# A graph-network kernel: three units of a weight combination are moved, one stage's tile order is changed, and the first loads are dealt out anew

## The reference, cut to what matters

```python
h = relu(layernorm(x)); x = x + gnn0(h, edges)          # attention, o, ff1, ff2
h = relu(layernorm(x)); x = x + gnn1(h, edges)          # lin, 2 x (sum neighbours, c1, c2)
h = relu(layernorm(x)); x = x + leaky(norm_adj @ (h @ W) + b)          # GCN
h = relu(layernorm(x)); x = x + rgcn(relu(rgcn(h)))     # relational, two layers
# in rgcn: w = einsum('rb,bio->rio', att, basis)        # 30 bases of 512x512 -> 2 weights, per layer
#          msgs_r = sigmoid(x_j @ gate_r) * x_j @ w[r];  out = segment_sum(...) + x @ root + bias
```

## Time and profile before

| | |
|---|---|
| median of 3 runs | 458.7 us (457.14 to 459.46) |
| the profiled execution | 456.62 us, its span from first to last instruction 454.8 us |
| busy in the span | PE 438.6 us, DVE 346.3, ACT 243.7, POOL 42.9 |
| granted TensorE clock, mean | 1.000 |

### The profile page before, as it was taken

How to read it: one execution, slowest core, us unless ns; L and a number is a source line. 1 busy time by engine, 2 the same in 40 slices (tenths; PEclk the granted TensorE clock), 3 DMA queues, 4 the chain that set the end, 5 groups by cost and what they waited for, 6 DMA issues and landing times.

```text
span 454.8 us, 6200 instructions
## 1 busy us (share of the span) xinstructions
PE 438.6 (96%) x2226; PEld 274.3 (60%) x2226; DVE 346.3 (76%) x736; ACT 243.7 (54%) x428; POOL 42.9 (9%) x59
## 2 busy tenths in 40 slices
PE   8999999899997899999999999999998999999997
PEld 3334554443432346768776866677465788888885
DVE  5999996899999968688779657675759695866212
ACT  5999994676897617543345436544534623511210
POOL 3240000024223011000010000010000000000000
PEclk9999999999999999999999999999999999999999
DMA  7997347426699859978099766777973550000002
GB/s 254 415 398 176 110 174 308 179 93 219 235 380 353 295 206 332 409 272 345 11 372 404 295 246 251 275 252 267 375 199 115 225 186 1 1 0 2 0 3 92
DMA packets 18090, 99.22 MB, mean 218 GB/s; under 512 B 2959, under 2 KB 3599, under 8 KB 7567
## 3 DMA queue, kind: packets, MB, share of 16 engines
q1 hardware_dynamic: 13191, 72.72, 43.4%
q0 software_dynamic: 4000, 25.18, 15.1%
q10 hardware_dynamic: 864, 0.86, 0.6%
HBM read 93.50 MB, written 5.25 MB: 217 GB/s over the span
## 4 chain that ended last, share of the span: by engine, by line
PE 70%; DVE 12%; DMA 8%; issue 8%; ACT 1%; POOL 0%; DVEq 0%; POOLq 0%
PE bank L1371 15%; PE sbank L1703 10%; PE bank L1716 6%; PE sbank L1357 6%; PE sbank L1427 6%; PE bank L1608 5%; DMA bring<-in_basis 4%; PE bank L1688 4%; PE sbank L1567 3%; PE bank L1450 3%; DMA wring<-in_weights 3%; PE bank L1357 3%; PE bank L1513 2%; PE sbank L1337 2%; PE sbank L1490 2%
## 5 line engine op out<-in xcount | busy, mean ns | idle before, releaser
L839 DVE TENSOR_SCALAR cnt<-iota_row,edge_f 128x512 bf16<-128x512 f16 x132 | 41.4, 350 | 0.4 <-PE sbank L1427 0.4
L1357 PE MATMUL sbank<-bring,attw 120*32 120x512 f32 x336 | 41.0, 599 | 0.1
L1427 PE MATMUL sbank<-cnt,adjT 128*128 128x512 bf16 x132 | 30.6, 380 | 0.3
L466 ACT ACTIVATE stat<-stat,eps 128x1 f32<-128x1 f32 x32 | 9.4, 294 | 39.3 <-DVE stat L858 39.3
L576 ACT ACTIVATE adjT<-distance,edge_w,edge_f 128x128 bf16<-128x128 bf16 x61 | 29.2, 479 | 1.4 <-PE sbank L1427 1.4
L1281 DVE SCALAR_TENSOR_TENSOR y_lo<-sbank,gate,y_hi 128x512 fp32r<-128x512 f32 x16 | 11.8, 750 | 22.6 <-ACT y_hi L765 22.5
L497 ACT ACTIVATE s<-bank,colsb 128x512 f32<-128x512 f32 x24 | 16.4, 687 | 21.8 <-PE bank L1371 21.8
L1427 PEld LDWEIGHTS sbank<-cnt,adjT 128*128 128x128 bf16 x132 | 12.3, 98 | 21.7 <-DVE cnt L839 6.4
L529 ACT ACTIVATE distance<-iota_row,edge_f 128x128 bf16<-128x128 f16 x61 | 24.3, 400 | 1.8 <-DVE edge_f L905 0.4
L1371 PE MATMUL bank<-hT_hi,w_hi 128*128 128x512 f32 x64 | 25.3, 395 | 0.0
L1371 PE MATMUL bank<-hT_hi,w_lo 128*128 128x512 f32 x64 | 24.9, 390 | 0.0
(11 more groups left out here) (250 smaller groups left out, 1092.5 us busy)
## 6 DMA issues: line engine op xcount, KB each, us to landing
bring<-in_basis SPq DMA_DIRECT2D x59, 1024.0 KB, 9.8
wring<-in_weights POOLq DMA_DIRECT2D x8, 1024.0 KB, 10.0
landing<-in_weights POOLq DMA_DIRECT2D x4, 1024.0 KB, 5.1
w_scratch<-stage SPq DMA_DIRECT2D x16, 256.0 KB
hT<-in_weights POOLq DMA_DIRECT2D x4, 1024.0 KB, 9.1
qkw<-w_scratch POOLq DMA_DIRECT2D x2, 2048.0 KB, 7.9
rring<-in_rows POOLq DMA_DIRECT2D x12, 256.0 KB, 8.5
wring<-in_basis SPq DMA_DIRECT2D x2, 1024.0 KB, 12.9
```

The source lines that it names most:

```text
L839: dve.tensor_scalar(hot_s[:, n % HOT, :], iota[:, :], src_f[:, n:n + 1], None, ALU.is_equal).then_inc(sem("hot_ready"), 1)
L1357: mm = pe.matmul(unit_bank(b)[32 * j:32 * j + 32, :], attw[0:KB, u // UNITS, g, :], unit_place(u)[0:KB, j, :], start=(g == 0), stop=(g == ...
L1427: pe.matmul(bank[7][:, :], hot_d[:, n % HOT, :], hot_s[:, n % HOT, :], start=(n == 0), stop=(n == ECH - 1)).then_inc(sem("hot_used"), 1)
```

## The change

Five edits. (1) SP loads all four tiles of x; ACT loads only `dst`, `src`, then `etype`. (2) DVE derives `dst_part`, `src_f` and `dst_lo` ahead of the norm statistics of x, waiting for the two loads; the rest stays behind the transposed copies. (3) The low parts of root1 are made by POOL (`low_parts`), right behind its load of root1, and no longer by DVE. (4) In attention steps 2 to 6 one of the three units stands between the pairs 0 and 1. (5) `units(5)` and the four matmuls of zeros become `units(6)`, so that units 60, 61 and 62 each come one place earlier and only unit 63 stays behind the first turn; and the gcn stage goes `BY_TILE`.

```diff
-                for c in (0, 2):
+                for c in range(C):
                     sp.dma_start(xr[:, c, :], x[:, c, :]).then_inc(sem(f"x{c}_loaded"), 16)
...
+                def low_parts(name, ks=range(C)):
+                    hi, lo = weight_parts(name)
+                    i = IN_PARTS.index(name)
+                    for k in ks:
+                        pool.wait_ge(sem("weight_hi"), i * C + k + 1)
+                        if i and k == 0:
+                            pool.wait_ge(sem("weight_parts"), i * C)
+                        pool.tensor_tensor(lo[:, k, :], weight(name)[:, k, :], hi[:, k, :].bitcast(F32),
+                                           ALU.subtract).then_inc(sem("weight_parts"), 1)
...
                 load_weight("root1")
+                low_parts("root1")
                 load_w(0)
...
-                for c in (1, 3):
-                    act.dma_start(xr[:, c, :], x[:, c, :]).then_inc(sem(f"x{c}_loaded"), 16)
-                for i, e in enumerate((src, dst, etype)):
+                for i, e in ((1, dst), (0, src)):
                     act.dma_start(edge_i[:, i, :], e).then_inc(sem("edges_loaded"), 16)
+                act.dma_start(edge_i[:, 2, :], etype).then_inc(sem("cols_loaded"), 16)
...
+                dve.wait_ge(sem("edges_loaded"), 32)
+                dve.tensor_scalar(dst_part[:, 0, :], edge_i[:, 1, :], P - 1, None, ALU.bitwise_and)...
+                dve.tensor_scalar(dst_part[:, 1, :], edge_i[:, 1, :], P.bit_length() - 1, None,
+                                  ALU.logical_shift_right)...
+                dve.tensor_copy(src_f, edge_i[:, 0, :]).then_inc(sem("edge_step"), 1)
+                dve.wait_ge(sem("edge_step"), 3)
+                dve.tensor_copy(dst_lo, dst_part[:, 0, :]).then_inc(sem("edge_step"), 1)
                 for c in range(C):
                     dve.wait_ge(sem(f"x{c}_loaded"), 16)
                     norm_stats(0, xr[:, c, :], c)
...
                 split_weight("gcn")
                 for c in range(C):
                     T_lo("agg2", c)
-                split_weight("root1")
...
                             products(it + 1, pair)
                             exclude(it + 1, pair, "scores_psum")
+                            if it >= 2 and pair == 0:
+                                units(1)
...
-                    units(STEP_UNITS[it])
+                    units(STEP_UNITS[it] - (1 if 2 <= it < 2 * C - 1 else 0))
...
-                units(5)
-                keep_clock(4, bank[4])
+                units(6)
...
-                parts_stage("gcn", hT_parts, "agg2", "gcn_psum", t_major=False)
+                parts_stage("gcn", hT_parts, "agg2", "gcn_psum", order=BY_TILE, t_major=False)
...
                 turn_rel(0, "h_rel0", 0)
-                units(2)
+                units(1)
```

More of the change, by code:

```diff
@@ L583, in _ @@
                         if t == 0:
-                            act.wait_ge(sem("cols_loaded"), 32)
+                            act.wait_ge(sem("cols_loaded"), 48)
                         qk_take(t)
@@ L875, in take_v @@
                     dve.tensor_tensor(vr[:, c, :], bank[v_bank(c)][:, :], row("bv"), ALU.add).then_inc(sem("v"), 1)
+                dve.wait_ge(sem("edges_loaded"), 32)
+                dve.tensor_scalar(dst_part[:, 0, :], edge_i[:, 1, :], P - 1, None, ALU.bitwise_and).then_inc(
+                    sem("edge_step"), 1)
+                dve.tensor_scalar(dst_part[:, 1, :], edge_i[:, 1, :], P.bit_length() - 1, None,
+                                  ALU.logical_shift_right).then_inc(sem("edge_step"), 1)
+                dve.tensor_copy(src_f, edge_i[:, 0, :]).then_inc(sem("edge_step"), 1)
+                dve.wait_ge(sem("edge_step"), 3)
+                dve.tensor_copy(dst_lo, dst_part[:, 0, :]).then_inc(sem("edge_step"), 1)
                 for c in range(C):
@@ L888, in _ @@
                                     bank[c][:, :].rearrange("p (f n) -> p f n", f=C)).then_inc(sem("hT0"), 1)
[L890 to L895, removed]
+                dve.wait_ge(sem("cols_loaded"), 48)
                 dve.tensor_scalar(rel1, edge_i[:, 2, :], 0.0, None, ALU.not_equal).then_inc(sem("edge_step"), 1)
-                dve.wait_ge(sem("edge_step"), 4)
-                dve.tensor_copy(dst_lo, dst_part[:, 0, :]).then_inc(sem("edge_step"), 1)
+                dve.wait_ge(sem("edge_step"), 5)
                 dve.scalar_tensor_tensor(field, rel1, float(C), dst_part[:, 1, :], ALU.mult, ALU.add).then_inc(
@@ L918, in _ @@
                         dve.tensor_scalar(never[:, :], ident[:, :], NEVER, None, ALU.mult).then_inc(sem("never_bq8"), 1)
-                        dve.wait_ge(sem("cols_loaded"), 32)
+                        dve.wait_ge(sem("cols_loaded"), 48)
                         dve.tensor_scalar(bq8[:, :], col("bq", 0, C), HD ** -0.5, None, ALU.mult).then_inc(
@@ L1476, in _ @@
                 NH = N // 2
-                pe.wait_ge(sem("cols_loaded"), 32)
+                pe.wait_ge(sem("cols_loaded"), 48)
                 def products(it, pair):
```

## The result

The changed kernel takes 468.3 us in the median (466.9 to 469.9, 4 runs), the kernel before 459.1 (457.1 to 459.6, 4 runs): a ratio of 1.020, with a 95% interval of 1.017 to 1.023. The forecast was 460.3, in a range of 456.1 to 462.3.

A forecast was written before the change was run, and what follows sets the result against it. The prediction took PE to bound the kernel almost everywhere, with DVE at the front, in attention and in the GCN stage. Front 0.85, attention 0.4 and GCN 0.3 summed to +1.55 us, 460.3 on the median, range 456.1 to 462.3.

The forecast's parts named there:

- a part comes back: Attention step 2: DVE's scaling, coming 0.9 later, no longer overlaps POOL's and takes 0.5 us less.
- net of +0.4: Attention: one unit's delay less the scaling's regained time costs +0.4 us, bounds -0.5 and +0.9.
- The delay of `find_max` by one unit: Attention step 2: pair 1 has no slack, so `find_max` moves by +0.9 us.
- The clock: Rival, GCN stage: PE's 3.1 us stand drops the clock to 1.2 GHz; sum +3.85, 462.6 us, chance 0.05.
- The price that I worked out for unit 60: GCN stage: with the clock at 1.2 GHz, unit 60 and the first aggregation quarter cost +2.3 us.
- The front: Start of kernel: `src` lands at 5.2, first one-hot +0.85 us, bounds -0.5 and +2.1.
- the rival of the late edges: Front: `src` lands at 6.5, front +2.1, sum +2.8, 461.5 us; decides from a 6.0 landing; chance 0.12.
- The GCN stage: PE waits for late slices; DVE's first gcn tile comes 2.2 us sooner, but that gain becomes a DVE wait.
- The forecast +0.3: GCN stage: net cost of +0.3 us, bounds -2.5 and +0.9.
- the alternative "-2.5": Rival, GCN stage: slices come in time, -2.5 us in place of +0.3, total 457.4 us, chance 0.18.
- PE's waits for bases: Attention: most of 3.8 us should go, costed at nothing; rival that they count: -2.3 there, 457.5 us, chance 0.09.

The follow-up runs named there:

- experiment 1: Kernel before with only the attention edit, one unit between pairs 0 and 1 in steps 2 to 6: 465.4 us, ratio 1.013.
- experiment 4: Kernel before with only the GCN changes: `units(6)` without the zeros, `BY_TILE`, root1's low parts on POOL: 459.6 us, ratio 1.004.
- experiment 12: Kernel before with the GCN changes, but thirteen matmuls of zeros between `units(5)` and unit 60: 458.0 us, ratio 1.000.
- experiment 3: Kernel before with only the front changes: x on one queue, edges on the other, edge fields ahead of the statistics: 460.2 us, ratio 1.006.
- experiment 5: Kernel before with root1's low parts on POOL and `BY_TILE`, units and zeros left in place: 456.0 us, ratio 0.995.
- experiment 8: Kernel before with a unit between the pairs only from attention step 3 on: 458.4 us, ratio 1.001.
- experiment 2: Changed kernel with the attention edit taken back: 462.9 us, ratio 1.012 against the kernel before.
- experiment 9: Changed kernel, all edits in, with POOL's scaling waiting for the end of `find_max`: 462.6 us, ratio 1.009 against the kernel before.

## Why the prediction was wrong

**What failed is the step "a part comes back" of attention, its net of +0.4 with the bounds -0.5 and +0.9.** The delay of `find_max` by one unit was right: DVE waited 1.00 us where 0.9 were forecast. I then looked only at DVE's scaling, which had overlapped POOL's, and counted 0.5 us back; it did come back (1.22 us at 118.53). I did not ask what else of DVE would move under POOL's 2.4 us. It was the last maximum, which had 0.55 us between its end and POOL's start (111.56 to 112.11), and the shift of 1.0 used it up. At full clock the step costs some 2.7 us, namely 1.0 of delay and 2.2 of a single held maximum, less the 0.5; the one run of experiment 1 at full clock is 2.3 above the median of the runs of before at full clock (457.6). The median of experiment 1, +7.5, lies above this, and its slower runs have the lower clocks; no run here fills that wait of PE, so the share of the clock in it is argued from the order of the runs.

The Trainium skill's rule of the exclusive pair ("SBUF — State Buffer", "SBUF: two separate sides") stood beside that very step, and the trace agrees with it: the held maxima, 0.42 us long by themselves, ended 0.3 us behind POOL's end, and DVE's scaling of before, 1.22 long, ended 1.08 behind it (115.58 against 114.50). I had used the rule for the gain, and not for the loss.

**The clock was given 0.05 and one place.** In the changed kernel's profiled execution it fell in three: behind the wait that the collision makes, behind that for the third projection, and behind that for unit 60. With the clock down PE was late once more, and the collision repeated; with the clock at full, in experiment 1, it did not. The price that I worked out for unit 60, 2.3 us, was measured as 1.6 (experiments 4 and 12). The warning of waits for a DMA in the Trainium skill ("TensorE: Matmul & The Clock Gate", "HAM oscillation — how this bites in real kernels") was right here, and the trace agrees: a wait of 3.4 us, then 0.50.

**The front** was right in kind and too small: a landing at 5.2 was taken, 6.0 measured, between the bounds; 0.85 us at the first one-hot were 1.6 in the changed kernel, 1.3 in experiment 3. So the rival of the late edges, which was to decide from 6.0 on, came true in the changed kernel, if only just, and its +2.1 was too much; in experiment 3 `src` landed at 5.67. The nearest row, a tile of x four times as large, was no guide to a small load's time.

**The GCN stage** went as described: PE stood until 10 us after the issue, the gain of DVE did not arrive. Two things in it differed. Counted from the issue of unit 59, DVE's first tile came 0.8 us sooner in the changed kernel and in experiment 4, and not 2.2: the fallen clock made PE late; in experiment 12, without the fall, it came 1.8 sooner. And L1264 and L1267 took 1.77 and 1.67 us beside POOL's low parts, in place of 0.69 each, so the spare time was spent there and not at the first L1238. The forecast +0.3 without the clock's fall agrees with experiment 12; the alternative "-2.5" was measured as -1.8 by experiment 5.

**PE's waits for bases** were rightly costed at nothing: they fell to 1.4 us, and nothing was won (experiment 8).

Left open: the load of `lin`, for which ACT waited 2.2 to 2.4 us in three of the fourteen profiles, that of before among them, and 5.6 to 6.4 in the other eleven, though no edit touches that stage. It is 1.5 us of the 13.3 between the two profiled executions and, as far as these runs tell, not of the change. The sum of the three edits alone, 7.5 + 2.3 + 1.6 = 11.4, is above the 9.3 measured, and experiment 2 above the sum of 3 and 4 by 1.0; where a wait lets the clock fall differs from run to run, and I have not settled this further. Nor do the parts explain the run of experiment 9 that is 4 us slow at full clock.

## What to carry to other kernels

When an edit moves an instruction of one engine by a microsecond, list everything on that engine in the next few microseconds against the other engine's long instructions, and not only the pair that overlapped before. A stretch in which PE has no wait hides more than its own time: each new wait of two or three microseconds can bring the clock down and be paid twice, and whether it does can differ between runs of one kernel. Before pulling a unit forward, add its load's measured time to its issue; here the rows of before showed that the slice would not be there, and the matmuls of zeros had a use.

## What the runs showed of the hardware that was not expected

How long PE waits does not by itself tell whether the clock falls. In the fourteen profiled executions all seven waits of 2.8 to 3.4 us were followed by a granted clock of 0.50; of the nine from 1.98 to 2.53 us five were; of the twenty-five from 1.28 to 1.89, the wait ahead of the first matmul left out, two were (1.33 in experiment 3, 1.89 in experiment 8). The wait of 2.22 us behind the held maximum was followed by a fall in the changed kernel and not in experiment 1, with PE busy ahead of it in both.

Either engine can be the one that is held when both work on SBUF alone: at 113.60 DVE started 0.02 behind POOL and took 2.62 in place of 0.42; at 124.69 it started 0.01 behind POOL by the trace, kept its 0.69, and POOL took 2.92 in place of 2.4.

A load of 66 KB, second on its queue behind one of its own size and beside four of 256 KB, took 4.8 us to land (4.4 to 4.9 in the five profiles that have it), longer than the 4.0 of the tile of x, 256 KB, that had been first on that queue before.
